# Rearranging the prologue and the borders of a three-pass macaron kernel

## The chip, the cores and the metric

One core of one Trainium2 chip runs the whole kernel in one launch. The metric is the device time of a launch in microseconds; lower is better. The kernel before takes 775.83 us (median of 3 runs, 775.14 to 775.91).

## The reference

x is 8192 rows (8 x 1024) of 256 float32. Three residual steps follow, each with a plain layer norm first, and each feed-forward step has a second layer norm with gamma and beta inside:

```
x = x + 0.5 * ffn(layernorm(x))
x = x + mixer(layernorm(x))
x = x + 0.5 * ffn(layernorm(x))          # same weights

ffn(r):   h = layernorm(r) * gamma + beta
          z = silu(h @ W1 + b1) @ W2 + b2            # W1 256x1024, W2 1024x256
          return r + 0.5 * z
          # W1, W2 = (q - 128) * scale, q int32, a scale for each 128 rows and each column
mixer(v): a = sigmoid(v Wa + ba); b = v Wb + bb; c = tanh(v Wc + bc)   # 64 wide
          s_t = a_t * s_(t-1) + (1 - a_t) * b_t      # a scan over 1024 rows of each batch entry
          return (c * s) Wy + by + v Wd + bd
```

## The kernel before

The rows are cut into 16 tiles (`NT`) of 512 rows, four blocks of 128 each (`SUB`), and x stays in on-chip memory (`resid`) for all three passes: feed-forward 1 over the 16 tiles, the mixer over the 16 tiles, feed-forward 2 over the 16 tiles. Each engine has an instruction stream of its own, written out by hand in program order; semaphores join them. The position of each piece of side work inside a tile is set by constants such as `STATISTICS_AT`, `TURN_AT`, `TURN_OUT_AT`, `LOWER_PART_AT` and `NORMALISE_AT`: they name the step f of the tile (0 to 7) at which it stands in its engine's stream.

A feed-forward tile has eight steps, one for each 128 columns of W1:

- TensorE (PE) computes `fc1` of step f (8 products into one of two PSUM bank pairs), then `fc2` of a group four steps back (`LAG`). Groups 0 and 1 are full-precision products (L838), the other six are products of a high and a low part (L808).
- ScalarE (ACT) makes u from the first half of the sum (L506) and the silu; VectorE (DVE) makes y from the second half (L630) and adds the z sums (L641). `fc1` of step f waits for y of step f - 2.
- GpSimd (POOL) makes the low parts `g_lo` (L394) and `h_lo` (L384), the `rsqrt` of the layer norms (L342 to L357), the normalised rows `xhat` (L365) and scales the residual (L375).
- TensorE turns xhat (L801) for the tile after; ScalarE takes it out of PSUM as h (L495, L500); the tile after may start `fc1` once its second `h_lo` is there. The sum z is turned back (L854) and added to the residual by VectorE (`add_ffn`, L649); the second turn back of a tile waits for the first addition, as both use one bank.

Before the first tile, x of tile 0 is loaded on the SP queue, ahead of a table of small vectors (`rows`), and q1 and q2 on ScalarE's. VectorE takes the statistics of tile 0, and then the largest absolute value of the converted weights (L728); it is turned on TensorE (L964) and becomes a flag that chooses between a program for narrow and one for wide integers. GpSimd normalises tile 0 alone, and in front of the first tile's work also tile 1. TensorE turns the table (L794), which ScalarE copies out as `cols`; three of its rows come by GpSimd's own queue.

In the mixer each tile has the a, b products (L808 with `wab_sb`), the c products, two turns for the tile after, the bias and Wd products (`d_products`, L897, L903), and the Wy products of the tile before (L911). VectorE runs `scan` (L759, L764) and c_sum (L776); TensorE's c products of a tile wait for c_sum of the tile before. The mixer's weights are split in high and low parts by `prepare_mixer` (L705 to L716) on VectorE, in step 3 of the first tile of all. The last mixer tile's products use the banks `ps_mix`, which are the `fc1` banks too.

In functions, `before` is 0 in the first tile of a pass, 1 in the second and 2 later; `behind` is how many tiles come after (3 for more). `ff0` is 0 in feed-forward 1 and 16 in feed-forward 2.

Of the kernel before, what the change touches and what calls it, by code (L numbers as in the profile page):

```python
# [5 lines left out]
ALU = mybir.AluOpType  # L6
# [6 lines left out]
P = 128  # L13
TILE = 512
SUB = TILE // P
LAG = 4
# [5 lines left out]
def macaron_kernel(nc, x, wa, ba, wb, bb, wc, bc, wd, bd, wy, by, gamma, beta,  # L22
# [23 lines left out]
    NORMALISE_AT = (5, 6)  # L46
    TURN_AT = (0, 2)
    TURN_OUT_AT = (((0, 0), 1), ((0, 1), 2), ((1, 0), 2), ((1, 1), 3))
    LOWER_PART_AT = (3, 4)
# [18 lines left out]
    with ExitStack() as ctx:  # L68
# [16 lines left out]
        largest = sb("largest", [P, 4])  # L85
# [48 lines left out]
        raw = resid[:, NT - 1, :, :].rearrange("p a d -> p (a d)")  # L134
        bias_raw = raw[:, 0:2 * D].rearrange("p (b d) -> p b d", b=2)
        wy_raw = raw[:, 2 * D:3 * D]
        wc_raw = raw[:, 3 * D:3 * D + KC * N].rearrange("p (k n) -> p k n", k=KC)
# [11 lines left out]
        x_loaded = [sem("x_loaded_even"), sem("x_loaded_odd")]  # L149
        rows_zero = sem("rows_zero")  # L150
        rows_loaded = sem("rows_loaded")
        mixer_rows_loaded = sem("mixer_rows_loaded")
        q1_loaded = sem("q1_loaded")
        q2_loaded = sem("q2_loaded")
# [25 lines left out]
        xhat_ready = sem("xhat_ready")  # L180
        resid_scaled = sem("resid_scaled")
# [72 lines left out]

        halves = (range(0, SUB // 2), range(SUB // 2, SUB))

# [20 lines left out]
        def _(sp):  # L277
            sp.dma_start(resid[:, 0, :, :], x_view[:, 0, :, :]).then_inc(x_loaded[0], 16)
            sp.wait_ge(rows_zero, 1)
            small = [(s1.rearrange("k (c p) -> (k c) p", p=P), R_S1, KC * FC),  # L280
                     (b1.rearrange("(c p) -> c p", p=P), R_B1, FC),
                     (s2.rearrange("g (n p) -> (g n) p", p=P), R_S2, FC * KC),
                     (b2.rearrange("(n p) -> n p", p=P), R_B2, KC),
                     (gamma.rearrange("(k p) -> k p", p=P), R_GAMMA, KC),
                     (beta.rearrange("(k p) -> k p", p=P), R_BETA, KC)]
            for src, r, n in small:
                sp.dma_start(rows[r:r + n, :], src).then_inc(rows_loaded, 16)
# [3 lines left out]
            for dst, src in ((wab_sb[:, :, 0:N], wa), (wab_sb[:, :, N:2 * N], wb), (wc_raw, wc),  # L291
                             (wd_sb[:, :, :], wd)):
                sp.dma_start(dst, src.rearrange("(k p) n -> p k n", p=P)).then_inc(mixer_loaded, 16)
# [8 lines left out]
            with sp.Fori(0, NT // 2 - 2) as i:  # L302
                for par in range(2):
                    sp.wait_ge(x_loaded[par], 16 * i + 16)
                    sp.dma_start(resid[:, 2 * i + (2 + par), :, :],
                                 x_view[:, 2 * i + (2 + par), :, :]).then_inc(x_loaded[par], 16)
            sp.wait_ge(mixer_ready, 1)
            for par in range(2):
                sp.wait_ge(x_loaded[par], 8 * NT - 16)
                sp.dma_start(resid[:, NT - 2 + par, :, :],  # L310
                             x_view[:, NT - 2 + par, :, :]).then_inc(x_loaded[par], 16)


            with sp.Fori(0, NT) as t:
                sp.wait_ge(ffn_added, 2 * t + (2 * NT + 2))
                sp.dma_start(out_view[:, t, :, :], resid[:, t, :, :]).then_inc(stored, 16)
            sp.wait_ge(stored, 16 * NT)

        @block.gpsimd
        def _(pool):  # L320
# [8 lines left out]
            nc.gpsimd.memset(bias_raw, 0.0).then_inc(raw_zero, 1)  # L329
# [29 lines left out]
            def normalise(ln, t, blocks=range(SUB)):  # L359
# [7 lines left out]
                if blocks[-1] == SUB - 1:  # L367
                    last.then_inc(xhat_ready, 1)

            def residual(ln, t, blocks=range(SUB)):  # L370

                if blocks[0] == 0:
                    pool.wait_ge(xhat_ready, ln + 1)
                for a in blocks:
# [42 lines left out]
            def feed_forward(ff0, ln0):  # L417
                def tile(t, par, before, behind):
                    ff, ln = t + ff0, t + ln0
                    for f in range(FC):  # L420
# [4 lines left out]
                        if f in LOWER_PART_AT:  # L425
# [574 lines left out]
```

## Time and profile before

| | us |
|---|---|
| median of 3 runs | 775.83 |
| time of the profiled execution | 776.82 |
| its span | 775.0 |
| PE busy | 733.0 (95%) |
| ScalarE busy | 659.0 (85%) |
| GpSimd busy | 644.0 (83%) |
| VectorE busy | 641.7 (83%) |

The profile is of one execution; its span runs from the first to the last instruction, and its time has some 1.8 us around that. Busy times are sums over instructions, weight loads not counted for PE. In a row of the timeline stand start, duration, engine, line, operation, output and inputs, shapes, and in brackets how long the engine had been idle and what ended it. PEclk in the windows is the granted clock of TensorE as a share of 2.4 GHz; it is shown as 1.00 up to the first recorded change (about 41.8 us), whatever it was.

### The profile page before, as it was taken

How to read it: one execution, taken by the hardware profiler on the slowest of the kernel's cores; microseconds unless marked ns; L12 is line 12 of the kernel's file. 1: busy time of each engine (PE TensorE's matmuls, PEld its weight loads, DVE VectorE, ACT ScalarE, POOL GpSimd, SP SyncE). 2: the span in 40 equal slices, each digit the busy share in tenths (PEclk: the TensorE clock that was granted, in tenths of full speed). 3: DMA queues.
4: the chain of work that ended last, by engine and by line, in shares of the span. 5: the costliest groups of instructions: out<-in, count | busy, mean ns of one | idle time of the engine just before them, and what ended most of it. 6: DMA issues, size and time to landing. Idle time of an engine off the chain costs nothing.

```text
span 775.0 us, 13958 instructions
## 1 busy us (share of the span) xinstructions
PE 733.0 (95%) x3234; PEld 547.0 (71%) x3234; DVE 641.7 (83%) x1244; ACT 659.0 (85%) x1113; POOL 644.0 (83%) x829
## 2 busy tenths in 40 slices
PE   1689999999999999989999997999999999999996
PEld 0467777777777776757877875677777777777774
DVE  3498898999999999668887783888999999999886
ACT  4579999999999998768888887999899999999984
POOL 5789999999999997748666685999999999999753
PEclk9999999999999999999999997999999999999999
DMA  8720000000000000000000000000000100000001
GB/s 265 239 86 0 2 0 0 1 0 0 0 0 0 1 1 1 1 0 2 0 0 0 1 0 2 0 29 28 28 27 33 48 28 27 27 28 28 28 28 57
DMA packets 19846, 20.24 MB, mean 26 GB/s; under 512 B 1574, under 2 KB 19420, under 8 KB 19804
## 3 DMA queue, kind: packets, MB, share of 16 engines
q1 hardware_dynamic: 18396, 17.66, 7.1%
q10 hardware_dynamic: 1312, 2.10, 0.8%
q8 instruction: 16, 0.26, 0.1%
q14 instruction: 26, 0.21, 0.1%
q0 software_dynamic: 96, 0.00, 0.0%
HBM read 11.37 MB, written 8.39 MB: 25 GB/s over the span
## 4 chain that ended last, share of the span: by engine, by line
PE 87%; issue 3%; DVE 3%; ACT 3%; POOL 2%; DMA 2%; DVEq 0%; ACTq 0%; POOLq 0%
PE ps_fc L808 30%; PE ps_z L808 27%; PE ps_z L838 13%; PE ps_fc L903 6%; PE ps_tr L801 4%; PE ps_tr L854 3%; PE ps_fc L911 2%; DMA q_int<-in_L_ffn_fc_q 2%; PE ps_fc L897 1%; DVE z_acc L641 1%; PE ps_z L801 1%; POOL rstd L351 0%; ACT g_native L523 0%; POOL cs_parts L413 0%; DVE stats L613 0%
## 5 line engine op out<-in xcount | busy, mean ns | idle before, releaser
L641 DVE SCALAR_TENSOR_TENSOR z_acc<-ps_z,cols,z_acc 128x512 f32<-128x512 f32 x384 | 276.5, 742 | 19.1 <-PE ps_z L808 17.2
L394 POOL TENSOR_TENSOR g_lo<-g_full,g_hi 128x512 fp32r<-128x512 f32 x192 | 248.6, 1295 | 44.3 <-ACT g_hi L528 40.7
L506 ACT ACTIVATE u_sb<-ps_fc,cols 128x512 f32<-128x512 f32 x256 | 199.7, 780 | 62.7 <-PE ps_fc L808 56.4
L630 DVE SCALAR_TENSOR_TENSOR y_sb<-ps_fc,cols,u_sb 128x512 f32<-128x512 f32 x256 | 190.2, 743 | 61.3 <-ACT u_sb L506 61.1
L808 PE MATMUL ps_fc<-h_hi,q_sb 128*128 128x512 f32 x512 | 229.5, 448 | 7.8 <-DVE y_sb L630 2.6
L808 PE MATMUL ps_fc<-h_lo,q_sb 128*128 128x512 f32 x512 | 203.8, 398 | 0.0
L808 PE MATMUL ps_z<-g_hi,q_sb 128*128 128x512 f32 x384 | 154.2, 401 | 1.4 <-DVE z_acc L641 1.0
L808 PE MATMUL ps_z<-g_lo,q_sb 128*128 128x512 f32 x384 | 151.5, 395 | 0.0
L526 ACT ACTIVATE g_full<-y_sb 128x512 f32<-128x512 f32 x192 | 120.0, 625 | 3.6 <-DVE y_sb L630 3.6
L808 PEld LDWEIGHTS ps_fc<-h_hi,q_sb 128*128 128x128 f32 x512 | 98.2, 192 | 35.0 <-issue 10.1
L838 PE MATMUL ps_z<-g_native,w_full 128*128 128x512 f32 x256 | 120.2, 591 | 0.0
L528 ACT ACTIVATE g_hi<-y_sb 128x512 fp32r<-128x512 f32 x192 | 120.1, 626 | 0.0
L808 PEld LDWEIGHTS ps_fc<-h_lo,q_sb 128*128 128x128 f32 x512 | 98.6, 193 | 23.3 <-issue 7.9
L808 PEld LDWEIGHTS ps_z<-g_hi,q_sb 128*128 128x128 f32 x384 | 72.5, 189 | 23.2 <-DVE z_acc L641 2.5
L808 PEld LDWEIGHTS ps_z<-g_lo,q_sb 128*128 128x128 f32 x384 | 72.4, 189 | 16.1
L384 POOL TENSOR_TENSOR h_lo<-h_full,h_hi 128x512 fp32r<-128x512 f32 x64 | 83.2, 1300 | 0.6 <-ACT h_hi L500 0.6
L613 DVE BATCH_NORM_STATS2 stats<-resid 128x6 f32 (+1 forms) x192 | 69.5, 410 | 9.0 <-DMA resid<-in_L_attn_x 9.0
L838 PEld LDWEIGHTS ps_z<-g_native,w_full 128*128 128x128 f32 x256 | 48.2, 188 | 36.4 <-issue 30.5
L351 POOL TENSOR_TENSOR rstd<-var_terms,minus_half 128x8 f32<-128x8 f32 (+1 forms) x48 | 69.7, 1452 | 4.0
L365 POOL TENSOR_SCALAR xhat<-resid,rstd,shift 128x256 f32<-128x256 f32 x128 | 71.2, 568 | 0.2
L375 POOL TENSOR_SCALAR resid<-resid,res_scale,shift 128x256 f32<-128x256 f32 x128 | 69.8, 562 | 1.0 <-ACT xhat L599 0.8
L801 PE MATMUL ps_tr<-ident,xhat 128*128 128x128 f32 x320 | 49.9, 280 | 12.8 <-POOL xhat L365 9.1
(91 smaller groups left out, 974.3 us busy)
## 6 DMA issues: line engine op xcount, KB each, us to landing
resid<-in_L_attn_x SPq DMA_DIRECT2D x16, 512.0 KB, 4.3
out_x<-resid SPq DMA_DIRECT2D x16, 512.0 KB, 2.9
q_int<-in_L_ffn_fc_q ACTq DMA_DIRECT2D x2, 1024.0 KB, 9.6
z_acc<-in_L_ffn_fc_scales SPq DMA_DIRECT2D x1, 256.0 KB, 7.2
wd_sb<-in_L_attn_Wd SPq DMA_DIRECT2D x1, 256.0 KB
resid<-in_L_attn_Wy SPq DMA_DIRECT2D x2, 64.0 KB
wab_sb<-in_L_attn_Wa SPq DMA_DIRECT2D x1, 64.0 KB
wab_sb<-in_L_attn_Wb SPq DMA_DIRECT2D x1, 64.0 KB
```

Of the source, the lines that this page charges most:

```text
L365: last = nc.gpsimd.tensor_scalar(xhat[:, a, :], resid[:, t, a, :], rstd[:, 0, a:a + 1], shift[:, 0, a:a + 1], ALU.mult, ALU.add)
L375: last = nc.gpsimd.tensor_scalar(resid[:, t, a, :], resid[:, t, a, :], res_scale[:, a:a + 1], shift[:, 1, a:a + 1], ALU.mult, ALU.add)
L384: nc.gpsimd.tensor_tensor(h_lo[:, par, c, :], h_full[:, c, :], h_hi[:, par, c, :].bitcast(F32), ALU.subtract).then_inc(h_ready, 1)
L394: nc.gpsimd.tensor_tensor(g_lo[:, slot, :], g_full[:, g % 2, :], g_hi[:, slot, :].bitcast(F32), ALU.subtract).then_inc(g_ready, 1)
L506: nc.scalar.activation(u_sb[:, f % 2, :], ps_fc1[:, f % 2, 0, :], ACT.Identity, bias=col(R_B1 + f), scale=col(R_S1 + f)).then_inc(u_ready, 1)
L526: nc.scalar.activation(g_full[:, g % 2, :], y_sb[:, g % 4, :], ACT.Silu)
L528: nc.scalar.activation(g_hi[:, split_slot(g, par), :], y_sb[:, g % 4, :], ACT.Silu).then_inc(g_hi_ready, 1)
L630: nc.vector.scalar_tensor_tensor(out=y_sb[:, f % 4, :], in0=ps_fc1[:, f % 2, 1, :], scalar=col(R_S1 + FC + f), in1=u_sb[:, f % 2, :], op0= ...
L641: nc.vector.scalar_tensor_tensor(out=z, in0=bank_of(g, n, par), scalar=col(R_S2 + KC * g + n), in1=z, op0=ALU.mult, op1=ALU.add).then_inc( ...
L801: last = nc.tensor.transpose(bank[:, a * P:(a + 1) * P], xhat[:, a, c * P:(c + 1) * P], ident[:, :])
L808: last = nc.tensor.matmul(out, w, v, start=start and i == 0, stop=stop and i == len(pairs) - 1)
L838: last = nc.tensor.matmul(bank_of(g, n, par), w2_full[:, g, at], g_native[:, g, :], start=g == 0, stop=g == NATIVE - 1)
```

## The change

- The SP queue loads x of tile 0 in two halves, then q1 and q2 in two pieces each with a semaphore for each piece, the scales, x of tiles 1, 2 and 3, and after them the mixer weights. The table of small vectors goes to ScalarE's queue, behind the clearing of the table. The mixer weights have buffers of their own.
- The largest value is sought in the integers as loaded, in four pieces, and compared with `WIDE - ZERO_POINT`; the conversion of q2 on ScalarE stands behind the first h.
- xhat of tile 0: GpSimd makes blocks 0 and 1, ScalarE blocks 2 and 3. GpSimd's rsqrt and xhat of the second tile of a pass stand in step 0 of the first tile, in both feed-forward passes; in the mixer's last tile GpSimd has no rsqrt and ScalarE no xhat.
- In the first two tiles of a pass turns, turns out, lower parts and xhat stand at other steps than later; the statistics of the third tile stand in step 3 and not 1.
- `prepare_mixer` is spread over step 4 of tiles 13, 14 and 15 of feed-forward 1 (three copies; two subtractions; one subtraction); `ones` is made at the start.
- TensorE multiplies the identity by itself 20 times after the turn of the table, and 10 times after the turns of tile 0.
- In the mixer's first tile c_sum stands ahead of drive and scan. Its last tile's products use two banks of `ps_z`; its Wy products stand in step 1 of the next pass, and the wait for their addition in step 4.
- The last tile is stored in two halves.

```diff
-    NORMALISE_AT = (5, 6)
-    TURN_AT = (0, 2)
-    TURN_OUT_AT = (((0, 0), 1), ((0, 1), 2), ((1, 0), 2), ((1, 1), 3))
-    LOWER_PART_AT = (3, 4)
+    NORMALISE_AT = ((6, 7), (5, 6), (5, 6))
+    TURN_AT = ((4, 5), (1, 3), (0, 2))
+    TURN_OUT_AT = ((((0, 0), 5), ((0, 1), 5), ((1, 0), 6), ((1, 1), 6)),
+                   (((0, 0), 2), ((0, 1), 3), ((1, 0), 4), ((1, 1), 4)),
+                   (((0, 0), 1), ((0, 1), 2), ((1, 0), 2), ((1, 1), 3)))
+    LOWER_PART_AT = ((6, 7), (4, 5), (3, 4))
+    WARM_UP = (20, 10)
...
+        def mix_bank(t, par, half):
+            if type(t) is int and t == NT - 1:
+                return ps_z[:, half, :]
+            return ps_mix[:, par, half, :]
...
         def _(sp):
-            sp.dma_start(resid[:, 0, :, :], x_view[:, 0, :, :]).then_inc(x_loaded[0], 16)
-            sp.wait_ge(rows_zero, 1)
...
+            sp.dma_start(resid[:, 0, 0:2, :], x_view[:, 0, 0:2, :]).then_inc(x_half_loaded, 16)
+            sp.dma_start(resid[:, 0, 2:4, :], x_view[:, 0, 2:4, :]).then_inc(x_loaded[0], 16)
+            for k in range(KC):
+                sp.dma_start(q1_int[:, k, :], q1[k * P:(k + 1) * P, :]).then_inc(q1_loaded[k], 16)
+            q2_view = q2.rearrange("(g p) d -> p g d", p=P)
+            for k, part in enumerate(q2_halves):
+                sp.dma_start(q2_int[:, part, :], q2_view[:, part, :]).then_inc(q2_loaded[k], 16)
...
+            for half in range(2):
+                blocks = slice(2 * half, 2 * half + 2)
+                sp.wait_ge(ffn_added, 4 * NT - 1 + half)
+                sp.dma_start(out_view[:, NT - 1, blocks, :], resid[:, NT - 1, blocks, :]).then_inc(stored, 16)
...
                         elif before:
                             g_low(ff - 1, FC - 1, 1 - par)
-                        if f in LOWER_PART_AT:
+                        else:
+                            rsqrt(ln0 + 1, True)
+                            normalise(ln0 + 1, 1)
+                        if f in lower_at:
...
                 if ff0 == 0:
                     rsqrt(ln0, True)
-                    normalise(ln0, 0)
+                    normalise(ln0, 0, halves[0])
                     residual(ln0, 0)
                     for c in range(KC):
                         h_low(ln0, ff0, 0, c)
-
-                    rsqrt(ln0 + 1, True)
-                    normalise(ln0 + 1, 1)
...
                 if before:
                     cs_low(t - 1, 1 - par)
-                twice = behind < 2
-                rsqrt(t + (NT + 2), twice)
+                if behind:
+                    rsqrt(t + (NT + 2), behind == 1)
...
         def _(act):
-            act.dma_start(q1_int[:, :, :], q1.rearrange("(k p) f -> p k f", p=P)).then_inc(q1_loaded, 16)
-            act.dma_start(q2_int[:, :, :], q2.rearrange("(g p) d -> p g d", p=P)).then_inc(q2_loaded, 16)
+            act.wait_ge(rows_zero, 1)
...
+            for src, r, n in small:
+                act.dma_start(rows[r:r + n, :], src).then_inc(rows_loaded, 16)
...
+            for k in range(KC):
+                act.wait_ge(q1_loaded[k], 16)
+                nc.scalar.activation(q1_sb[:, k, :], q1_int[:, k, :], ACT.Copy,
+                                     bias=-ZERO_POINT).then_inc(q1_ready, 1)
...
+                    normalise(ln0, 0, halves[1], xhat_half_ready)
...
-                normalise(t + (NT + 2), 1 - behind if behind < 2 else t + 2)
-                if not behind:
+                if behind:
+                    normalise(t + (NT + 2), 0 if behind == 1 else t + 2, range(SUB), xhat_ready)
+                else:
...
-                        if ff0 == 0 and not before and f == 3:
-                            prepare_mixer()
-                        if not before and f == 1:
+                        if ff0 == 0 and f == STATISTICS_AT[0]:
+                            prepare_mixer(behind)
+                        if not before and f == 3:
...
+                    for k in range(KC):
+                        largest_of(k, q1_int[:, k, :], q1_loaded[k])
+                    for k, part in enumerate(q2_halves):
+                        largest_of(KC + k, q2_int[:, part, :].rearrange("p g d -> p (g d)"), q2_loaded[k])
...
-                scan(t, par)
+                if before:
+                    scan(t, par)
                 dve.wait_ge(c_part_ready, t + 1)
                 nc.vector.tensor_tensor(c_sum, ps_c[0:N, :], c_part, ALU.add).then_inc(c_sum_ready, 1)
+                if not before:
+                    scan(t, par)
...
+                        if ff0 and not before and f == LAG:
+                            pe.wait_ge(mix_added, 2 * NT)
...
-                        if ff0 and not before and f == 0:
+                        if ff0 and not before and f == 1:
                             y_products(NT - 1, 1)
-                            pe.wait_ge(mix_added, 2 * NT)
...
+            def warm_up(count):
+                for _ in range(count):
+                    nc.tensor.matmul(ps_fc1[:, 0, 0, 0:P], ident[:, :], ident[:, :], start=True, stop=True)
+
+            warm_up(WARM_UP[0])
             pe.wait_ge(cols_ready, 1)
+            pe.wait_ge(xhat_half_ready, 1)
             for c in range(KC):
                 turn(0, c, (ps_tr, ps_tr2)[c], 2)
-            pe.wait_ge(largest_found, 3)
+            warm_up(WARM_UP[1])
+            pe.wait_ge(largest_found, 5)
```

## Rows read from the trace of the kernel before

**Rows 1.** Windows: stretch, its length, busy (records) of PE, PEld, DVE, ACT, POOL, PEclk, DMA
```profile
42.00:44.00 2.00, 2.00 (x6) 1.29 (x6) 1.73 (x9) 2.00 (x5) 1.35 (x2) 0.50 0.84 266
...
100.00:240.00 140.00, 140.00 (x617) 104.70 (x615) 126.99 (x236) 128.55 (x216) 130.67 (x172) 1.00 0.00 0
...
474.00:476.00 2.00, 2.00 (x6) 1.58 (x5) 0.00 (x0) 0.56 (x1) 0.00 (x0) 0.50 0.00 0
```

**Rows 2.** Timeline, all engines, start to the first product
```profile
7.24 1.91 ACT L482 ACTIVATE q_sb<-q_int 128x2048 fp32r<-128x2048 int32 x1 [3.92 <-DMA q_int<-in_L_ffn_fc_q]
...
7.85 1.40 DVE L613 BATCH_NORM_STATS2 stats<-resid 128x6 f32<-128x256 f32 x4 [7.85 <-DMA resid<-in_L_attn_x]
...
9.77 0.20 POOL L342 TENSOR_SCALAR var_terms<-mean_var 128x4 f32<-128x4 f32 x1 [5.77 <-DVE mean_var L623]
...
9.89 0.31 PE L794 MATMUL ps_z<-ident,rows 48*128 48x48 f32 x1 [9.89 <-DMA rows<-in_L_attn_bc]
...
15.14 1.09 PE L801 MATMUL ps_tr<-ident,xhat 128*128 128x128 f32 x4 [4.94 <-POOL xhat L365]
...
17.85 2.59 POOL L384 TENSOR_TENSOR h_lo<-h_full,h_hi 128x512 fp32r<-128x512 f32 x2 [0.58 <-ACT h_hi L500]
...
18.27 0.14 DVE L739 TENSOR_SCALAR wide_flag<-largest 1x1 int32<-1x1 f32 x1
...
19.59 1.41 DVE L613 BATCH_NORM_STATS2 stats<-resid 128x6 f32<-128x256 f32 x4 [1.18 <-DMA resid<-in_L_attn_x]
...
20.50 0.80 PE L808 MATMUL ps_fc<-h_hi,q_sb 128*128 128x512 f32 x1 [2.58 <-POOL h_lo L384]
```

**Rows 3.** Timeline, all engines, the first tile of feed-forward 1
```profile
21.51 0.20 POOL L342 TENSOR_SCALAR var_terms<-mean_var 128x4 f32<-128x4 f32 x1 [1.07 <-DVE mean_var L623]
...
24.52 2.19 POOL L365 TENSOR_SCALAR xhat<-resid,rstd,shift 128x256 f32<-128x256 f32 x4
...
37.34 1.32 POOL L384 TENSOR_TENSOR h_lo<-h_full,h_hi 128x512 fp32r<-128x512 f32 x1
...
37.45 1.49 DVE L713 TENSOR_TENSOR wy_lo<-resid,wy_hi 128x256 fp32r<-128x256 f32 x1
...
38.95 1.66 DVE L714 TENSOR_TENSOR bias_parts<-resid,bias_parts 2x512 fp32r<-2x512 f32 x1
...
41.44 0.50 PE L808 MATMUL ps_fc<-h_hi,q_sb 128*128 128x512 f32 x1 [2.28 <-DVE y_sb L630]
...
46.87 0.39 PE L808 MATMUL ps_fc<-h_hi,q_sb 128*128 128x512 f32 x1
```

**Rows 4.** Timeline, PE and DVE, steps 5 and 6 of tile 14, feed-forward 1
```profile
295.60 1.88 PE L838 MATMUL ps_z<-g_native,w_full 128*128 128x512 f32 x4
...
296.62 0.75 DVE L630 SCALAR_TENSOR_TENSOR y_sb<-ps_fc,cols,u_sb 128x512 f32<-128x512 f32 x1 [0.79 <-ACT u_sb L506]
...
298.36 0.66 DVE L649 SCALAR_TENSOR_TENSOR resid<-ps_tr,resid 128x512 f32<-128x512 f32 x1
...
299.62 0.60 PE L854 MATMUL ps_tr<-ident,z_acc 128*128 128x128 f32 x4
```

**Rows 5.** Timeline, the border from feed-forward 1 to the mixer
```profile
335.28 0.69 DVE L649 SCALAR_TENSOR_TENSOR resid<-ps_tr,resid 128x512 f32<-128x512 f32 x1 [0.81 <-PE ps_tr L854]
...
338.54 0.47 PE L808 MATMUL ps_z<-h_hi,wc_parts 128*128 128x512 f32 x1 [1.58 <-DVE q_int L776]
```

**Rows 6.** Timeline, the border from the mixer to feed-forward 2
```profile
464.97 2.08 ACT L599 ACTIVATE xhat<-resid,shift,rstd 128x256 f32<-128x256 f32 x4 [1.24 <-POOL shift L357]
...
467.48 0.47 PE L808 MATMUL ps_fc<-h_hi,q_sb 128*128 128x512 f32 x1 [1.83 <-issue]
...
468.46 0.61 ACT L593 ACTIVATE cs_parts<-q_int 64x512 fp32r<-64x512 f32 x1
...
489.10 0.39 PE L808 MATMUL ps_fc<-h_hi,q_sb 128*128 128x512 f32 x1
```

**Rows 7.** DMA issues: count, KB each, median us from issue to landing
```profile
out_x<-resid SPq DMA_DIRECT2D x16, 512.0 KB, 2.9
```

More of the change, by code:

```diff
@@ L419, in tile @@
                     ff, ln = t + ff0, t + ln0
+                    lower_at, normalise_at = LOWER_PART_AT[before], NORMALISE_AT[before]
                     for f in range(FC):
@@ L500, in affine, with normalise @@
                     nc.scalar.activation(h_hi[:, par, c, :], h_full[:, c, :], ACT.Copy).then_inc(h_hi_ready, 1)
+            def normalise(ln, t, blocks, signal):
+                act.wait_ge(shift_ready, ln + 1)
+                wait(act, turned, 2 * ln)
+                for a in blocks:
+                    last = nc.scalar.activation(xhat[:, a, :], resid[:, t, a, :], ACT.Identity,
+                                                bias=shift[:, 0, a:a + 1], scale=rstd[:, 0, a:a + 1])
+                last.then_inc(signal, 1)
             def first_group(step, f):
@@ L549, in tile @@
                             silu(ff - 1, FC - 1, 1 - par)
-                        for (c, rounded), at in TURN_OUT_AT:
+                        for (c, rounded), at in TURN_OUT_AT[before]:
                             if at != f:
@@ L593, in mixer_tile @@
                 nc.scalar.activation(cs_parts[0:N, par, :], cs_full, ACT.Copy).then_inc(cs_hi_ready, 1)
-            def normalise(ln, t):
-                act.wait_ge(shift_ready, ln + 1)
-                act.wait_ge(turned, 2 * ln)
-                for a in range(SUB):
-                    last = nc.scalar.activation(xhat[:, a, :], resid[:, t, a, :], ACT.Identity,
-                                                bias=shift[:, 0, a:a + 1], scale=rstd[:, 0, a:a + 1])
-                last.then_inc(xhat_ready, 1)
             for c in range(KC):
@@ L679, in tile @@
                                 dve.wait_ge(x_loaded[1 - par], 8 * t + (32 if par == 0 else 40))
+                            if not before and f == STATISTICS_AT[0]:
+                                dve.wait_ge(aggr_done, ln0 + 3)
                             statistics(t + 3 if behind >= 3 else 2 - behind, halves[STATISTICS_AT.index(f)])
@@ L948, in mixer_tile @@
                 for half in range(2):
+                    if before == 2 and not behind:
+                        pe.wait_ge((b_ready, c_sum_ready)[half], NT)
                     d_products(t, par, half)
```

144 lines of the change are left out of this document (76 added, 68 removed).

## The prediction, made before the change was run

> **What bounds the kernel now.** I read the windows first: in the steady part of a feed-forward pass TensorE (PE) is busy 140.00 of 140 us [rows 1], so a gain can come only from the ends and from the borders between passes. Second the timeline of the first 47 us. TensorE's first product starts at 20.50, held by GpSimd's two h_lo instructions (17.85 + 2.59), behind the turn of xhat at 15.14, GpSimd's rsqrt from 9.77 and xhat, and the statistics, which wait for x until 7.85 [rows 2]. The row table arrives last: its turn on TensorE runs at 9.89 [rows 2]. The second tile starts at 46.87 [rows 3], 26.4 us after the first; a steady tile takes 18.2 (80 records of TensorE a tile, 617 in 140 us) [rows 1], and the first has less to do. VectorE is held there by the mixer preparation, the last two of whose three subtractions fill 37.45 to 40.61 [rows 3]. Third the borders: between feed-forward 1 and the mixer TensorE waits 1.58 us for VectorE's c_sum [rows 5]; into feed-forward 2 its first product is at 467.48, when GpSimd has finished h_lo, and the second tile's at 489.10, 21.6 us later, part of it at the granted clock 0.50, the 1.2 GHz level [rows 1, 6].
>
> **Part 1, start to first product.** x and the integers now stand in one queue, x first and in halves; before, x shared the engines with q1. 0.5 MB of x and 1 MB of q1 were in by 7.85 [rows 2]. Alone in front x lands by about 4.4: its issue ends at some 1.5, and 512 KB take 2.9 in a quiet queue [rows 7]. Statistics and variance take 1.9 (7.85 to 9.77) [rows 2]: done by 6.3. GpSimd's rsqrt and shift take 3.0 (21.51 to 24.52, tile 1) [rows 3]: 9.3. Its half of xhat is 1.1 (half of 2.19) [rows 3], 10.4. ScalarE's half stands behind the row table's columns (about 10) and the q1 cast (1.91) [rows 2], plus some 1.0: xhat is whole at about 12.8, against 15.1 now.
>
> TensorE does not take it up then. Its 20 warm-up products stand in order between the turn of the table and the turns of xhat. A full-precision product has two records; with 512 columns they lie 0.43 apart at 2.4 GHz (four in 1.88, less the tail) [rows 4], so with 128 columns 0.107 each: 0.21 a product at the upper level, 0.43 at the lower, where the engine starts (four turns take 1.09 at 15.14; such a turn is 0.60 to 0.63 in steady tiles) [rows 2, 4]. Twenty cost 4.3 to 8.5; starting cold, partly warm, I take 6.8. The table's turn I put at 9.2, a little earlier than 9.89, since its rows no longer stand behind x; ends 6.0 and 9.9. So TensorE is free at 16.0, and turns xhat. From the end of the first turn to the first product the old chain takes 4.3 (16.23 to 20.50) [rows 2]: 16.5 + 4.3 = 20.8, plus 0.2 for the flag. The flag now stands behind 10 more warm-up products (2.1) and lands at about 20.0, and reading it costs the time from 18.27 to VectorE's next work at 19.59, 1.2 or so [rows 2]: 21.0 as well. First product 21.0, 0.5 late.
>
> The Trainium skill (DMA: Bandwidth & Descriptors, Queues, rings and completion order) says that a DMA engine takes turns between its queues packet by packet. By it GpSimd's three 256-byte rows would come in soon after issue, whatever the others carry; it is the rival of early rows below. The table's turn at 9.89, though the last of them was issued at 3.5, speaks against it [rows 2].
>
> **Part 2, first tile of pass 1.** Without the 5.3 us of mixer preparation, TensorE, ScalarE and VectorE are through with the tile by about 37. What is late next is GpSimd. In its order now stand: rsqrt of tile 1 (3.0: 21.51 to 24.52), xhat (2.2), residual (four blocks like xhat's, 2.2), rsqrt of tile 2 (3.0) [rows 3], five g_lo and two h_lo of 1.3 (2.59 for two) [rows 2], half an xhat, 1.1. Sum 20.6, all of it ahead of the second h_lo, because LOWER_PART_AT is (6, 7) in the first tile; before, h_lo stood at groups 3 and 4. The chain starts when statistics of tile 1 are done, which VectorE takes after the flag: 21.0 + 1.9 = about 23.0. So the second tile starts at 43.6, 3.3 earlier than 46.87 [rows 3]. But TensorE has then been idle for some 6 us. After a gap of 2.3 us (ending 41.44) [rows 3] the granted clock is 0.50 in 42 to 44, and in pass 2 it still is in 474 to 476 [rows 1]; I let the tile start at 1.2 GHz for 5 us, which gives back half of that, 2.5. Ends: none, and 3.4, from a low start of nearly 7 us. Net -0.8; ends -3.3 and +1.0. Two loads on SP moved ahead of the mixer weights cost nothing: the weights are wanted some 250 us later.
>
> **Part 3, preparation moved to tiles 13, 14 and 15.** In the before trace a subtraction ends just after a GpSimd instruction does: h_lo 37.34 + 1.32 = 38.66, the subtraction that began at 37.45 at 38.94 [rows 3]; the third, on 2 partitions, still took 1.66. So each costs one GpSimd instruction, 1.3. In those tiles GpSimd is as full. The slack at the new place is VectorE's 0.79 before the next y [rows 4] and 0.6 between the residual sum (298.36 + 0.66) and the turn back at 299.62 that waits for it [rows 4]. Tile 14: two subtractions, 2.6 - 1.4 = 1.2. Tile 15: one, 1.3 - 1.4, nothing. Tile 13: three copies, which in the old place fell where GpSimd had small instructions alone, and fitted before the subtractions; between 0 and 3 x 1.3 - 1.4 = 2.5 I take the middle, 1.2. TensorE is the bound there, so nothing of this comes back. Together +2.4; ends 0 and 6.2.
>
> The Trainium skill (SBUF — State Buffer, Who interferes with whom) has VectorE and GpSimd share a pair of ports, exclusively, for copies in a two-port mode and for subtractions with two inputs in SBUF. By it all three copies would wait and this part would cost 3.7; the trace agrees for the subtractions and shows nothing for the copies.
>
> **Part 4, border into the mixer.** c_sum moves ahead of drive and scan. TensorE stood 1.58 until 338.54 for it [rows 5]; its inputs are there and VectorE is free at 336.0 (335.28 + 0.69) [rows 5], so it ends by 336.7, before TensorE arrives at 337.0, and the wait goes; tanh and xhat on ScalarE move up as much. What is late next is the state, 0.7 later in VectorE's order, which the copy of cs on ScalarE takes only after xhat. -1.6; ends 0 and -1.8.
>
> **Part 5, border into pass 2.** GpSimd's h_lo no longer waits for an rsqrt, so the first product comes straight after the mixer's last ones, 1.8 before 467.48, at 465.6 [rows 6]; the last mixer products move to banks of their own and stop nobody. But GpSimd's order in the tile is that of part 2: it starts behind the last cs_lo. The copy of cs before that, at 468.46, loses ScalarE's wait of 1.24 and its xhat of 2.08 ahead of it [rows 6] and comes at 465.2, its 0.6 and GpSimd's 1.3 end at 467.3 with the gaps, and 20.6 later, 487.9, the second tile starts: 1.2 before 489.10 [rows 6]. TensorE has idled some 5 us and begins low: +2.5, less 0.3 for a small wait that was there. Net +1.0; ends -1.5 and +2.2.
>
> **Part 6, the end.** The last store is cut in two. One of 512 KB lands in 2.9 us [rows 7]; the second half has 256 KB. -0.6; ends 0 and -1.0. The remaining edits (ones made at the start, six columns of maxima, four shorter reductions on integers in place of two) lie beside the loads or inside the wait of part 1: 0.
>
> **Sum**: -0.8 + 2.4 - 1.6 + 1.0 - 0.6 = +0.4. The span of 775.0 becomes 775.4, and the profiled execution 776.82 becomes 777.2; the three runs have their median 1.0 below that execution, 775.83. Forecast 776.2, own range 773.9 to 778.4.
>
> **Rivals.**
> - The clock stays up. If TensorE's gap in the two first tiles is short (GpSimd done sooner, the products later) or the level holds, 2 x 2.5 goes: 771.2. For it: GpSimd's sum is made of rows measured beside a full VectorE; against: the low stretch after 2.3 us of idling.
> - The rows arrive early, at 6. Then the warm-up ends at 12.9, as early as xhat, and the chain of part 2 is 3.1 earlier: 773.1. For it: fewer bytes before them in their queue; against: GpSimd's three, which were in a queue of their own before too.
> - Slower: the preparation at its full price. Each copy waits, the subtractions wait from the start of a GpSimd instruction, and VectorE, without slack outside groups 4 and 5, carries the delay on: 6.2 in place of 2.4, 780.0. It decides from the point where VectorE is more than 1.4 us late at group 5 of a tile.
> - The border into the mixer gives nothing, as the change intends it to, because ScalarE or the state is the wait behind c_sum: 777.8.
>
> **Chances.** Forecast 0.42, clock 0.20, early rows 0.13, preparation 0.15, border 0.10. 0.2% is 1.55 us and is about what a measurement can tell from none: faster means under 774.3, slower over 777.4. Faster: 0.19 of the clock case, 0.11 of early rows, 0.08 of the forecast's own range, 0.38. Slower: 0.14 of the preparation, 0.06 of the border, 0.10 of the forecast's, 0.30. Same 0.32. The range goes from just below the clock case, 770.5, to the preparation's, 780.0.
>
> **What would show it.** Right: TensorE's turns of tile 0 only after the warm-up, near 16; first product near 21; second tile near 43.6, released by GpSimd's h_lo, at granted clock 0.50; VectorE's late y and a wait of the turn back in tiles 13 and 14; no wait for c_sum; the second tile of pass 2 released by h_lo. Wrong: a second tile before 42 or at full clock, turns that start as soon as xhat is there, or tiles 13 to 15 as long as their neighbours.

## The result, and the profile after

| | before | after |
|---|---|---|
| median (4 runs each) | 775.49 (774.51 to 775.91) | 786.92 (785.89 to 788.25) |
| profiled execution, its span | 776.82, 775.0 | 788.25, 786.4 |
| PE busy | 733.0 (95%) | 744.2 (95%) |

The ratio is 1.0145 (95% interval 1.0129 to 1.0161): 11.4 us slower, where 776.2 was forecast. The result lies outside the range.

The kernel after was timed in this set alone, and the kernel before again with each set of experiments: its medians are 775.49 to 775.85, so a difference from the kernel after that is taken by medians below carries up to some 0.4 us of that.

Where the 11.4 us are is read by one event that both traces have in every tile, VectorE's y of step 0 (L630 before, L656 after); between two tiles without trouble both kernels take 18.2 us. The table is of one execution each.

| from, to (start of y of step 0) | before | after | difference |
|---|---|---|---|
| start, tile 0 of pass 1 | 23.42 | 24.50 | +1.07 |
| tile 0, tile 1 | 25.82 | 27.19 | +1.37 |
| tile 1, tile 3 | 36.80 | 38.60 | +1.82 |
| tile 3, tile 13 | 182.09 | 182.10 | 0 |
| tile 13, tile 15 | 36.44 | 41.00 | +4.56 |
| tile 15, tile 0 of pass 2 (the whole mixer) | 165.21 | 161.06 | -4.15 |
| tile 0, tile 1 of pass 2 | 21.70 | 28.04 | +6.33 |
| tile 1, tile 3 of pass 2 | 37.38 | 38.51 | +1.14 |
| tile 3, last y | 233.93 | 233.96 | +0.03 |
| last y, end of span | 12.21 | 11.44 | -0.77 |

Two rows of it hold something that is not the change. The first y comes at 23.30 to 24.59 us in the eight profiled kernels that share this prologue (24.50 is near the upper end), mostly because the 20 identity products took 6.31 to 7.60 us. And this execution of the kernel before has a stretch of 10.2 us at the granted clock 0.50 at the border into pass 2 (468.5 to 478.7), which the same border in e6 below doesn't have; tile 0 to tile 1 of pass 2 takes 20.04 there, not 21.70.

The windows of the kernel after, in the columns of [rows 1]: the steady part is as full as before, the two first tiles run in part at the lower level of the clock (0.50), and tiles 13 and 14 have lost 2.6 us of TensorE.

```profile
36.00:43.00 7.00, 4.87 (x14) 4.02 (x15) 1.19 (x2) 5.64 (x10) 2.72 (x4) 0.53 0.80 227
...
50.00:53.00 3.00, 3.00 (x9) 2.29 (x8) 1.98 (x3) 1.82 (x3) 0.88 (x2) 0.52 0.01 3
...
100.00:240.00 140.00, 140.00 (x622) 104.93 (x620) 126.66 (x240) 128.42 (x216) 130.73 (x169) 1.00 0.00 0
...
280.00:310.00 30.00, 27.36 (x112) 19.56 (x111) 27.54 (x51) 23.08 (x39) 24.39 (x28) 0.94 0.00 1
...
484.00:504.00 20.00, 12.28 (x33) 9.53 (x33) 7.22 (x16) 10.35 (x17) 12.63 (x15) 0.66 0.00 0
```

The timeline of the kernel after, from the table's turn to the first product; it answers to [rows 2].

```profile
9.92 0.31 PE L839 MATMUL ps_z<-ident,rows 48*128 48x48 f32 x1 [9.92 <-DMA rows<-in_L_attn_bc]
10.16 7.49 PE L1011 MATMUL ps_fc<-ident 128*128 128x128 f32 x40
...
12.27 1.08 ACT L527 ACTIVATE xhat<-resid,shift,rstd 128x256 f32<-128x256 f32 x2
...
17.49 0.60 PE L846 MATMUL ps_tr<-ident,xhat 128*128 128x128 f32 x4
...
22.46 0.49 PE L853 MATMUL ps_fc<-h_hi,q_sb 128*128 128x512 f32 x1 [1.59 <-POOL h_lo L397]
```

xhat is whole at 13.35 and its turn starts at 17.49, when the identity products are through. The first tile, in the columns of [rows 3], the three engines in order of time:

```profile
24.45 0.20 POOL L353 TENSOR_SCALAR var_terms<-mean_var 128x4 f32<-128x4 f32 x1 [0.96 <-DVE mean_var L649]
...
29.73 2.16 POOL L388 TENSOR_SCALAR resid<-resid,res_scale,shift 128x256 f32<-128x256 f32 x4
...
32.78 1.64 POOL L362 TENSOR_TENSOR rstd<-var_terms,minus_half 128x8 f32<-128x8 f32 x1
...
34.82 3.85 POOL L407 TENSOR_TENSOR g_lo<-g_full,g_hi 128x512 fp32r<-128x512 f32 x3
...
36.17 0.63 ACT L555 ACTIVATE g_full<-y_sb 128x512 f32<-128x512 f32 x1 [2.92 <-POOL g_lo L407]
...
37.22 0.76 ACT L515 ACTIVATE h_full<-ps_tr,cols 128x512 f32<-128x512 f32 x1
...
38.13 1.09 PE L846 MATMUL ps_tr<-ident,xhat 128*128 128x128 f32 x4 [3.98 <-ACT h_full L515]
...
42.85 1.29 POOL L407 TENSOR_TENSOR g_lo<-g_full,g_hi 128x512 fp32r<-128x512 f32 x1 [4.19 <-ACT g_hi L557]
...
47.67 1.25 POOL L397 TENSOR_TENSOR h_lo<-h_full,h_hi 128x512 fp32r<-128x512 f32 x1
...
48.98 0.50 PE L853 MATMUL ps_fc<-h_hi,q_sb 128*128 128x512 f32 x1 [4.14 <-POOL h_lo L397]
```

This is read backwards. The second tile waits for h_lo at 48.98; GpSimd is late with it because it stood 4.19 us for g_hi of a later group; that is late because TensorE stood 3.98 us in its second turn for h_full; ScalarE came to h_full late because the silu of group 4 ahead of it waited 2.92 us for g_lo of group 2 (`g_full` has two buffers); and that g_lo stood behind the rsqrt of the third tile. The first tile of pass 2 has the same picture; its first product comes straight after the mixer's last one.

```profile
472.33 0.58 PE L853 MATMUL ps_fc<-h_hi,q_sb 128*128 128x512 f32 x1
...
486.02 0.63 ACT L555 ACTIVATE g_full<-y_sb 128x512 f32<-128x512 f32 x1 [2.83 <-POOL g_lo L407]
...
487.99 1.09 PE L846 MATMUL ps_tr<-ident,xhat 128*128 128x128 f32 x4 [3.89 <-ACT h_full L515]
...
498.86 0.79 PE L853 MATMUL ps_fc<-h_hi,q_sb 128*128 128x512 f32 x1 [3.83 <-POOL h_lo L397]
```

Tile 13 in the kernel after, where [rows 4] had room: VectorE's three copies lie against GpSimd's instructions, and TensorE's turn back waits.

```profile
280.54 1.30 POOL L397 TENSOR_TENSOR h_lo<-h_full,h_hi 128x512 fp32r<-128x512 f32 x1
281.12 0.80 DVE L743 CAST wc_parts<-wc_raw 128x128 fp32r<-128x128 f32 x1
281.79 1.28 POOL L407 TENSOR_TENSOR g_lo<-g_full,g_hi 128x512 fp32r<-128x512 f32 x1
281.85 1.38 DVE L744 CAST wy_hi<-wy_raw 128x256 fp32r<-128x256 f32 x1
...
283.02 1.35 POOL L397 TENSOR_TENSOR h_lo<-h_full,h_hi 128x512 fp32r<-128x512 f32 x1
283.14 1.51 DVE L745 CAST bias_parts<-bias_raw 128x512 fp32r<-128x512 f32 x1
...
287.77 0.63 PE L899 MATMUL ps_tr<-ident,z_acc 128*128 128x128 f32 x4 [1.95 <-DVE resid L675]
```

### The profile page after: what moved, and what is told of

The parts are those of the page before. It is cut to its first block, busy times and chain, and to the rows that moved or that the text cites. A ratio compares the mean times of both kernels' runs of the same rounds, so it can differ in the third digit from the quotient of the medians.

```text
span 786.4 us, 14080 instructions
## 1 busy us (share of the span) xinstructions
PE 744.2 (95%) x3294; PEld 557.6 (71%) x3294; DVE 645.1 (82%) x1246; ACT 659.2 (84%) x1112; POOL 642.4 (82%) x831
## 4 chain that ended last, share of the span: by engine, by line
PE 83%; POOL 5%; issue 4%; DVE 3%; ACT 3%; DMA 1%; DVEq 0%; ACTq 0%; POOLq 0%
PE ps_fc L853 28%; PE ps_z L853 25%; PE ps_z L883 12%; PE ps_fc L949 7%; PE ps_tr L846 4%; PE ps_tr L899 3%; PE ps_fc L957 2%; PE ps_fc L1011 1%; POOL h_lo L397 1%; PE ps_fc L943 1%; POOL rstd L362 1%; DVE stats L639 1%; DMA rows<-in_L_attn_bc 1%; POOL xhat L376 1%; PE ps_z L846 1%
## 5 line engine op out<-in xcount | busy, mean ns | idle before, releaser
L656 DVE SCALAR_TENSOR_TENSOR y_sb<-ps_fc,cols,u_sb 128x512 f32<-128x512 f32 x256 | 190.4, 744 | 46.5 <-ACT u_sb L535 46.3
L853 PE MATMUL ps_z<-g_hi,q_sb 128*128 128x512 f32 x384 | 155.9, 406 | 1.1 <-DVE z_acc L667 1.1
L853 PE MATMUL ps_z<-g_lo,q_sb 128*128 128x512 f32 x384 | 153.4, 399 | 0.0
```

The costliest lines, as they stand in the source:

```text
L656: nc.vector.scalar_tensor_tensor(out=y_sb[:, f % 4, :], in0=ps_fc1[:, f % 2, 1, :], scalar=col(R_S1 + FC + f), in1=u_sb[:, f % 2, :], op0= ...
L853: last = nc.tensor.matmul(out, w, v, start=start and i == 0, stop=stop and i == len(pairs) - 1)
```

## The experiments

After each measured median stand, in brackets, its ratio to the kernel before and the 95% interval of the ratio.

The theory at this point had three losses: **G**, GpSimd's order in the two first tiles, which reaches TensorE through ScalarE's silu; **P**, two or three preparation instructions in one step; **W**, the identity products. The border into the mixer was thought to be a gain.

### First set: one part at a time

**e1_turn_out_at_4**, the turn out ahead of the silu that waits:

```diff
-    TURN_OUT_AT = ((((0, 0), 5), ((0, 1), 5), ...
+    TURN_OUT_AT = ((((0, 0), 4), ((0, 1), 5), ...
```

> The changed kernel with one constant different: in the first tile of both feed-forward passes ScalarE takes the first turned half out at step 4, ahead of the silu of group 4, and not at step 5 behind it. Theory S (waits in series): in the changed kernel the silu of group 4 waits for a g_lo that GpSimd makes only after its long chain, the turn out stands behind it, and TensorE's second turn (idle 3.98 in pass 1, 3.89 in pass 2) behind that; then both waits go, the second tile of the passes starts at about 45.1 and 494.9 in place of 48.98 and 498.86, and the time is about 779. Rival G (GpSimd's work alone): the second tile starts when GpSimd's sum is through, wherever the turn out stands: no more than 1 us is gained, 786 to 787.

Measured: 783.75 (ratio to before 1.0100, 1.0072 to 1.0127). This lies between what Theory S (about 779) and Rival G (786 to 787) expected. TensorE's second turn no longer waits, yet the median is only 3.2 us lower; by the traces it is 4.3, of which 1.0 is an earlier first product. The silu waits as long as it did, and TensorE now waits for what comes of it:

```profile
35.33 0.63 ACT L555 ACTIVATE g_full<-y_sb 128x512 f32<-128x512 f32 x1 [3.05 <-POOL g_lo L407]
```
```profile
38.20 0.79 PE L853 MATMUL ps_z<-g_hi,q_sb 128*128 128x512 f32 x1 [2.17 <-ACT z_acc L543]
...
46.07 0.79 PE L853 MATMUL ps_fc<-h_hi,q_sb 128*128 128x512 f32 x1 [3.81 <-POOL h_lo L397]
```

So the turn out carried the wait and was not its source.

**e3_prepare_in_tile_0**, the whole preparation behind the variance in step 5 of the first tile:

```diff
                             if f == STATISTICS_AT[1]:
                                 variance(ln + 3)
+                                if ff0 == 0 and not before:
+                                    prepare_mixer()
```

> The changed kernel with the whole mixer preparation back in the first tile of all, at step 5 behind the statistics, where VectorE idles from 35 to 41.8. Theory P (the moved preparation costs where it now stands): tiles 13 to 15 run as long as their neighbours, which gives back the 4.56 us that y of tile 15 falls behind there; in the first tile VectorE's six instructions fit into its idle time, though they hold up GpSimd's g_lo by their own length, 0 to 1.5. Time 782.5 to 783.5. Rival (the first tile has no room for it, as in the kernel before, where it cost TensorE 2.3 us and the clock): the first tile loses 3 or more, 785.5 to 787.

Measured: 784.71 (1.0115, 1.0097 to 1.0134), short of what Theory P expected (782.5 to 783.5). In the trace tiles 13 to 15 take 18.2 us each again, all 4.56 us back, and the first three tiles are 0.7 longer. By the profiled executions it is 3.6 us shorter than the kernel after, by the medians 2.2.

**e5_no_warm_up**:

```diff
-    WARM_UP = (20, 10)
+    WARM_UP = (0, 0)
```

> The changed kernel without the 30 products of the identity with itself. Theory W (they stand in the way): TensorE's turns of tile 0 begin when xhat is whole, 13.4 in place of 17.49, the first product at about 18.5 in place of 22.46 though at 1.2 GHz, and as GpSimd's order sets the second tile, that comes 2.5 to 4 earlier: 783 to 784.5. Rival (the raised clock pays for them): the first tile is slower by what the start gains, 786 to 788.

Measured: 784.43 (1.0106, 1.0073 to 1.0139), where Theory W expected 783 to 784.5. The four runs lie far apart (781.85 to 786.58) and the interval overlaps that of the kernel after (1.0129 to 1.0161), so the times alone don't decide it; the trace does for the start. The first product comes 4.1 us earlier, at the lower level (0.79 against 0.49 for its first record), and GpSimd's chain gives 2.7 of it on:

```profile
13.08 1.09 PE L846 MATMUL ps_tr<-ident,xhat 128*128 128x128 f32 x4 [3.21 <-ACT xhat L527]
...
18.38 0.79 PE L853 MATMUL ps_fc<-h_hi,q_sb 128*128 128x512 f32 x1 [3.15 <-POOL h_lo L397]
```

**e6_before_c_sum_first**, the kernel before with one part of the change:

```diff
+                if before:
                     scan(t, par)
                 dve.wait_ge(c_part_ready, t + 1)
                 nc.vector.tensor_tensor(c_sum, ps_c[0:N, :], c_part, ALU.add).then_inc(c_sum_ready, 1)
+                if not before:
+                    scan(t, par)
```

> The kernel before with only this edit: in the mixer's first tile c_sum stands ahead of drive and scan. My step: the wait of 1.58 us goes and nothing takes its place: 773.9, 1.6 under the kernel before. Rival: the state, now later, or ScalarE's order holds the same place: 775.5, no change.

Measured: 773.73 (0.9982, 0.9967 to 0.9996), as expected (773.9). TensorE's product that waited 1.58 us [rows 5] starts at 337.01, straight behind the one before it:

```profile
335.82 1.45 PE L811 MATMUL ps_z<-q_int,wab_sb 128*128 128x512 f32 x3
337.01 0.49 PE L811 MATMUL ps_z<-h_hi,wc_parts 128*128 128x512 f32 x1
```

### Second set: the source of each loss

**e2_rsqrt_at_4**:

```diff
-                            if f == RSQRT_AT:
+                            if f == (RSQRT_AT if before else 4):
                                 rsqrt(ln + 2, twice)
```

> The changed kernel, with one thing moved: in the first tile of each feed-forward pass GpSimd's rsqrt of the third tile stands in step 4, behind g_lo of groups 2 and 3, not in step 2 ahead of them. Theory G (GpSimd's order in that tile is the missed wait: ScalarE's silu of group 4 waits 2.92 us for g_lo of group 2, which stands behind the 2.9-us rsqrt): the silu comes 2.9 us earlier in both passes, the stall of 3.98 us in TensorE's second turn becomes about 1, the clock stays up there, and the time is 787 - 2 x (2 to 3) = 781 to 783. Rival R (the rsqrt only moves the delay on, to g_lo of group 4 and with it to the silu of group 6 and the two h_lo): 785.5 to 788.

Measured: 779.04 (1.0046, 1.0032 to 1.0059), 7.9 us below the kernel after, from an order of six small instructions. That is 2 us more than Theory G expected (781 to 783): each pass gives 4 us and not 2 to 3. By the traces it is 9.3, of which 1.2 is an earlier first product (21.27 against 22.46; the identity products took 6.31 against 7.49). The three places that stood 2.92, 3.98 and 4.19 us, in this kernel:

```profile
32.09 0.63 ACT L555 ACTIVATE g_full<-y_sb 128x512 f32<-128x512 f32 x1
```
```profile
34.05 0.63 PE L846 MATMUL ps_tr<-ident,xhat 128*128 128x128 f32 x4 [1.09 <-ACT h_full L515]
...
43.64 0.80 PE L853 MATMUL ps_fc<-h_hi,q_sb 128*128 128x512 f32 x1 [5.26 <-POOL h_lo L397]
```
```profile
36.16 2.66 POOL L407 TENSOR_TENSOR g_lo<-g_full,g_hi 128x512 fp32r<-128x512 f32 x2
38.78 1.27 POOL L397 TENSOR_TENSOR h_lo<-h_full,h_hi 128x512 fp32r<-128x512 f32 x1
```

The silu and GpSimd no longer wait. From y of tile 0 to y of tile 1 it takes 23.97 us in pass 1 (27.19 after, 25.82 before) and 23.85 in pass 2 (28.04, 21.70), and GpSimd's chain alone is what is left: the second tile starts at 43.64, the 43.6 of the prediction. TensorE was through 5.26 us before that, at 38.4; in the kernel after it was through at 44.8 (48.98 less its wait of 4.14).

**e4_rsqrt_4_turn_out_4**, both edits.

> The changed kernel with both edits: rsqrt of the third tile in step 4 and the first turn out of the first tile in step 4. If the two are one chain (the turn waits for the turn out, the turn out for the silu, the silu for g_lo), each edit alone already opens it and both give what the better one gives: 781 to 783. If the silu also holds back the z sums and the later steps by itself, they add: 778 to 780.5. By Rival R nothing beyond the 783.8 of the turn out alone: 783 to 785.

Measured: 780.01 (1.0050, 1.0031 to 1.0069). The number falls in the band that was written down for "they add" (778 to 780.5), but that band took the rsqrt alone to give 781 to 783, and it gave 779.04. What decides is the comparison with e2: the turn out adds nothing to the rsqrt (780.01 against 779.04, with overlapping intervals; tile 0 to tile 1 takes 23.84 and 23.71 us in the two passes against 23.97 and 23.85). So it is one chain, its source in GpSimd's order.

**e7_prepare_one_per_step**; a call of `prepare_mixer` here issues one of the six instructions, in their old order:

```diff
-                        if ff0 == 0 and f == STATISTICS_AT[0]:
-                            prepare_mixer(behind)
+                        if ff0 == 0 and f in (3, 4):
+                            prepare_mixer(behind, f - 3)
```

> The changed kernel with the same six instructions of the mixer's preparation in the same three tiles, but one in step 3 and one in step 4 of each of tiles 13, 14 and 15, where VectorE is idle for 0.6 and 0.8 us, and not three, two and one in step 4. Theory P (it costs because two or three stand in one step and together outlast the idle time, so that TensorE's turn back waits and its clock falls): four of the 4.6 us that the three tiles lost come back, 782.5 to 783.5. Rival (each of the six waits for a GpSimd instruction and costs its 0.8 to 1.5 us wherever it stands): 786 to 788.5.

Measured: 782.43 (1.0085, 1.0066 to 1.0103). From tile 13 to tile 15 each tile takes 18.2 us. VectorE in tiles 13 and 14, and the window that answers to the one of the kernel after (27.36 us of TensorE there):

```profile
279.32 0.88 DVE L742 CAST wc_parts<-wc_raw 128x128 fp32r<-128x128 f32 x1
...
280.79 0.73 DVE L744 CAST wy_hi<-wy_raw 128x256 fp32r<-128x256 f32 x1
...
297.54 1.08 DVE L746 CAST bias_parts<-bias_raw 128x512 fp32r<-128x512 f32 x1
...
299.21 0.72 DVE L749 TENSOR_TENSOR wc_parts<-wc_raw,wc_parts 128x128 fp32r<-128x128 f32 x1
```
```profile
280.00:310.00 30.00, 30.00 (x134) 22.44 (x134) 29.26 (x58) 27.02 (x46) 27.39 (x32) 1.00 0.00 1
```

The same six instructions cost nothing when none has a second one behind it in its step. Theory P holds: the rival expected 786 to 788.5. How much of the 4.6 us is waiting and how much the clock, the run doesn't separate, since both go at once.

**e8_second_border_as_before**, the core of the edit; ScalarE's xhat in the mixer's last tile comes back in the same way, and `sched` picks the steps of turns, turns out, lower parts and xhat:

```diff
-                if behind:
-                    rsqrt(t + (NT + 2), behind == 1)
+                rsqrt(t + (NT + 2), behind < 2)
...
+                    sched = 2 if ff0 else before
-                        else:
+                        elif ff0 == 0:
                             rsqrt(ln0 + 1, True)
                             normalise(ln0 + 1, 1)
```

> The changed kernel with the border into the third pass as before: rsqrt and xhat of its second tile stand in the mixer's last tile again (GpSimd and ScalarE), and its first tile has the steps of the kernel before. The bank of the last mixer tile, its products in step 1 and the wait in step 4 stay as changed. Theory G: the 21.7 us between the first y of the third pass and that of its second tile come back (28.0 now), against some 2.3 us that the border itself had gained: 787 - 6.3 + (0 to 2.3) = 780.5 to 783. Rival (the long second step comes from the products in step 1 or the wait in step 4): 785.5 to 788.

Measured: 778.06 (1.0034, 1.0023 to 1.0045), 8.9 us below the kernel after. From tile 15 to tile 3 of pass 2 it takes 218.2 us, where the kernel after takes 227.6, the one before 224.3 and the one before with c_sum first 220.8. So it is also 2.6 us quicker than the old border: what is kept of the changed one, the banks, the products in step 1 and the wait in step 4, is what is left to pay for it. That is by elimination; no run has these parts alone. The windows are ten us at the first y of pass 2 (469.78, 468.25 and 475.52): the kernel before, then e6 with the same old border, then this one.

```profile
468.00:478.00 10.00, 7.84 (x25) 5.71 (x24) 3.88 (x8) 4.29 (x9) 3.45 (x5) 0.52 0.01 2
```
```profile
468.00:478.00 10.00, 6.60 (x30) 4.73 (x31) 5.77 (x15) 5.92 (x11) 5.19 (x9) 1.00 0.01 3
```
```profile
476.00:486.00 10.00, 8.54 (x37) 5.76 (x37) 7.04 (x19) 9.33 (x16) 7.69 (x14) 1.00 0.00 2
```

e6 has no stretch at 0.50 there, so the old border alone doesn't bring the 0.52 of the kernel before, and the 2.6 us are not the clock: at 1.00 in both, TensorE is busy for 6.60 us in e6 and 8.54 here. e6 has waits of 1.39 us for cs_parts (468.95) and 0.93 us for the addition (471.07); this kernel has neither there, and one of 1.23 us for y (480.98).

### Third set: do they add?

**f1_three_repairs** joins e2's edit (in pass 1 alone) with those of e7 and e8.

> The changed kernel with three repairs: in the first tile of feed-forward 1 the rsqrt of the third tile in step 4, the mixer's preparation one instruction per step in tiles 13 to 15, and the second border's rsqrt, xhat and first tile as before. If the three losses are separate and add, as the theory has them: the rsqrt alone gave 7.9 us for two passes, of which the trace puts 4.2 before the mixer (3.2 in the first tile; 1.2 of the 4.2 is an earlier first product, which differs between runs), the preparation 4.5, the border 8.9, so 786.9 - (3 to 4.2) - 4.5 - 8.9 = 769.3 to 770.5, 5 to 6 us below the kernel before. Rival (they overlap, two of them curing one stall): 772 to 776.

Measured: 769.91 (0.9918, 0.9903 to 0.9933), inside the 769.3 to 770.5 of the sum and outside the rival's 772 to 776. They add.

**f2_and_no_warm_up** takes WARM_UP = (0, 0) besides.

> The same with no identity products (0, 0 in place of 20, 10). Theory W (the 20 products end at 17.5 us, when the turns of tile 0 could have run at 14 to 15, and what they give the clock is worth less): 2 to 3 us below the run with the three repairs, 766.5 to 768.5. Rival (they pay once the first tile no longer stalls elsewhere, since the first products then run at half clock): equal or up to 2 us above it.

Measured: 768.54 (0.9902, 0.9884 to 0.9919). The first y is 2.1 us earlier and the span 2.2 shorter, but the intervals of the two overlap. From y of tile 0 to y of tile 1 the two kernels take 23.94 and 23.95 us. So no gain from the identity products was measured, here or in e5; how much they cost is not shown.

**f4_xhat_behind_h_lo**:

```diff
+                            first = not before and ff0 == 0
+                            if first:
+                                if f == 7:
+                                    normalise(ln + 2, t2)
-                            if f in normalise_at:
+                            elif f in normalise_at:
```

> The same as the kernel with no identity products, and in the first tile of feed-forward 1 both halves of GpSimd's xhat of the third tile stand in step 7 behind the second h_lo, not half in step 6 and half in step 7. Theory G (the second tile waits for GpSimd's chain alone): its first product comes 1.1 us earlier, the time of the half, and the kernel ends 0.5 to 1.5 us below that one, 765.5 to 767.5. Rival (the second tile's own turn then waits for xhat, or h_hi is what is late): equal.

Measured: 767.66 (0.9890, 0.9872 to 0.9908), the same as f2. The half of xhat is gone from the chain, and GpSimd waits for ScalarE's g_hi in its place (0.52 us in the row below), so the second tile starts at 42.00 (42.08 in f2). The rival's "equal" was right, though the late one is g_hi and not the turn or h_hi that it named.

```profile
39.47 1.26 POOL L407 TENSOR_TENSOR g_lo<-g_full,g_hi 128x512 fp32r<-128x512 f32 x1 [0.52 <-ACT g_hi L561]
```

**f3_changed_border_kept** has e2's edit in both passes, e7's, no identity products, and the changed border.

> The changed kernel with the rsqrt of the third tile in step 4 in both passes, the preparation one instruction per step, no identity products, and the second border as changed. If all add: 779.0 - 4.5 - (2 to 3) = 771.5 to 772.5, still below the kernel before, and 4 to 5 us above the one with the border as before. Rival (the changed border is as good once GpSimd's order is mended): within 1.5 us of that one, 766.5 to 769.5.

Measured: 772.53 (0.9952, 0.9933 to 0.9970). Even mended, the changed border is 4.0 us dearer than the mixed one of f2. f2 and f4 beat both kernels, the one before by 1.0%.

## Why the prediction was wrong

**Parts 1 and 2, first tile of pass 1: forecast -0.8, measured +4.3.** Part 1 was near in each step: the table's turn at 9.92 (9.2), the identity products 7.5 (6.8), xhat whole at 13.35 (12.8), the first product at 22.46 (21.0). In the eight profiled kernels with this prologue the identity products take 6.31 to 7.60 us and the first product is at 21.27 to 22.55, so the 6.8 was inside the scatter and the 21.0 just under it. The step that failed is the one of part 2 that has TensorE, ScalarE and VectorE "through with the tile by about 37", so that GpSimd's sum of 20.6 runs without a wait. TensorE was through at 44.8. From the rsqrt at 24.45 to the second tile at 48.98 it took 24.5: the 20.6, and 4.2 of waiting. I had listed what stands behind GpSimd's instructions for the second tile, not who inside the first tile waits for each: g_lo of group 2 frees the buffer of group 4. With that one order changed the chain ran as summed (23.31 to 43.59 in e2, 20.3 us), and the three stretches of parts 1 and 2 came to 0.8 us below the kernel before, the forecast. The clock at 0.50 behind the gap was foreseen, but there were two such stretches in this part: TensorE's 3.98 us brought one more.

**Part 3, preparation: +2.4, measured +4.6** (3.3 in tile 13, 1.3 in tile 14). The term for tile 13's copies was mis-sized: between 0 and 2.5 I took the middle, and the tile lost 3.3, more than the upper end. TensorE's wait there was 1.95 us, inside 0 to 2.5; the 3.4 us at the clock 0.50 behind it, up to 1.7 us by my estimate (half of them), were at nothing in the term. Each copy ended 0.1 to 0.3 us behind a GpSimd instruction, as the subtractions do. Tile 14's 1.2 was right, as was tile 15's 0. By the rule of the Trainium skill (SBUF — State Buffer, Who interferes with whom), which would have made 3.7 of this part, the copies wait too; the trace agrees with it, at 1.38 and 1.51 us for copies that fill a GpSimd instruction each. The rival with the full price (6.2) had the right mechanism and was dearer than what came; its 6.2 is not worked out there (six instructions of 1.3 us less the 1.4 of slack are 6.4).

**Part 4, into the mixer: -1.6**, right: e6 shows the wait gone and 1.8 us less in its median (interval 0.3 to 2.6), -1.9 in the trace from tile 15 to tile 0 of pass 2.

**Part 5, into pass 2: +1.0.** Parts 4 and 5 come to -4.15 + 7.47 = +3.3 together, against the -0.6 forecast. The border itself was 0.6 better than forecast: the first product stands straight behind the mixer's last (472.33, no gap). It comes 158.9 us after y of tile 15, where it was 162.9: 4.0 earlier, and parts 4 and 5 had 1.6 and 1.8. The failure is part 2's again: rsqrt at 474.31, second tile 24.5 us later, the same waits of 2.83 and 3.89. e2 takes 4.2 us off this tile by the one order, which leaves parts 4 and 5 at -0.9, against the forecast's -0.6. There is some luck in so near a number: the kernel before ran 10.2 us of this border at 0.50, which it doesn't always do. Against e6 or e8, whose clock stays up, e2's border is 2.6 and 5.2 us dearer: GpSimd's chain for the second tile, which before lay beside the mixer's last tile, is not free even with the order mended.

**Part 6, the end: -0.6**, measured -0.8. The halves of the last store land in 2.3 us where the whole took 2.9 [rows 7].

The sum was off by 11.0 us: 5.1 in parts 1 and 2, 2.2 in part 3, 3.9 in parts 4 and 5. By e2's trace the missed chain gives 8.0 of them (3.9 in pass 1, 4.1 in pass 2), part 3 gives 2.2, and the rest, about 1, is the later first product, which is within the scatter of this prologue. Of the rivals' signs, the early rows were wrong (9.92) and the clock did not stay up; the one slower rival was a different loss from the main one, and no case held the chain through ScalarE. The range was too narrow above for that reason: it carried the price of each part, but not the case that one wait goes round the engines and brings others.

What stays open: how e3's last 1 to 2 us are spread, the true price of the identity products, which of the parts kept at the border (banks, products in step 1, wait in step 4) pays, and why the clock falls at the old border in one execution and not in another.

## What to carry to other kernels

When work is put ahead of an in-order helper engine's stream, go through everything behind it and ask for each instruction which buffer it frees and who wants that next, not only who wants its result: 2.9 us of rsqrt ahead of one g_lo cost 4 us in each pass by way of ScalarE and TensorE, and moving it back two steps gave 7.9. Small instructions that queue against the helper are free one at a time in a step's idle time, and cost when they stand together. Take a compound change apart and keep the halves that pay: here the product banks, the products in step 1 and c_sum first, with the old tile order at the second border and the preparation one instruction per step, beat both kernels. And before a border is judged by one trace, look whether the clock fell in it: with the same instructions there, the kernel before, with a low stretch, took 21.70 us from tile 0 to tile 1 of pass 2, and e6, without one, 20.04.

## What the runs showed of the hardware

- TensorE's wait of 1.95 us in tile 13 of the kernel after (287.77) was followed by a stretch at 0.50 of 3.4 us, in a pass where it is otherwise full (280 to 310: mean 0.94). In e7, without the wait, the window from 280 to 310 has 1.00.
- The length of a wait did not settle it alone. At the border into pass 2 TensorE waits 1.83, 0.94 and 0.78 us in the kernel before, and the clock is 0.50 from 468.5 to 478.7; in e6 it waits 1.82, 1.39, 0.93 and 1.22 us at the same border and the clock stays at 1.00.
- The same 20 identity products took 6.31 to 7.60 us in eight kernels with the same prologue.
- Without identity products the four turns took 1.09 us and the first product's first record 0.79 (0.60 and 0.49 with them): the engine was at the lower level, in f2 until 22.6 us. From y of tile 0 to y of tile 1 f2 takes 23.94 us and f1, with them, 23.95, since the second tile waits for GpSimd's h_lo in both.
- VectorE's three copies took 0.22 to 0.42 us in the kernel before beside small GpSimd instructions, and a subtraction 0.41 in e3 with GpSimd idle; beside GpSimd's 1.3-us instructions copies and subtractions took 0.72 to 1.51 (kernel after and e7).
